# A fused vision tower on one core: order of the queues in the second attention layer

## The reference, cut to what matters

```python
qkv = x @ W_qkv + b_qkv
dots = jnp.einsum('bhid,bhjd->bhij', q, k) * dk ** (-0.5)
dots = dots * mask.astype(dots.dtype)
attn = jax.nn.softmax(dots, axis=-1)
out_attn = jnp.einsum('bhij,bhjd->bhid', attn, v)
out_attn = out_attn.transpose(0, 2, 1, 3).reshape(b, n, e) @ W_out + b_out
...
return w[0] * out_attn + w[1] * x_cema
```

## Time and profile before

| what | value |
|---|---|
| median of 3 runs | 828.24 us (827.29 to 828.71) |
| profiled execution, its own time | 827.36 us |
| its span in the trace | 825.6 us |
| busy: PE, DVE, ACT, POOL | 76%, 61%, 42%, 28% of the span |
| second attention in the trace | 589.5 to 749.9 us |

### The profile page before, as it was taken

One profiled execution on the slowest core, in us unless ns is written; L12 is line 12 of the kernel. 1 busy time (PEld: TensorE's weight loads), 2 busy tenths in 40 slices (PEclk: granted clock), 3 DMA queues, 4 the chain that ended last, 5 costly groups with the idle time before them and its releaser, 6 DMA issues. The chain is left out here.

```text
span 825.6 us, 21280 instructions
## 1 busy us (share of the span) xinstructions
PE 630.7 (76%) x8455; PEld 513.7 (62%) x8455; DVE 504.3 (61%) x904; ACT 348.7 (42%) x871; POOL 230.8 (28%) x254
## 2 busy tenths in 40 slices
PE   2999999999999996761399867858689999971002
PEld 1888888888888885541394546638567777761001
DVE  0376666666666666427222678759578888855862
ACT  0013444444444444422164333443167888865600
POOL 1263333333333333000000223330235555430001
PEclk9999999999999998665558997775579999995555
DMA  8443333333332300003980440000000000001300
GB/s 358 161 191 119 118 119 117 117 117 117 117 117 117 117 2 2 2 1 106 198 116 0 54 52 0 0 2 0 1 2 4 0 0 0 3 2 53 74 5 4
DMA packets 28659, 55.36 MB, mean 67 GB/s; under 512 B 12274, under 2 KB 25698, under 8 KB 26114
## 3 DMA queue, kind: packets, MB, share of 16 engines
q1 hardware_dynamic: 28515, 54.62, 22.1%
q0 software_dynamic: 96, 0.07, 0.0%
HBM read 48.14 MB, written 6.55 MB: 66 GB/s over the span
## 5 line engine op out<-in xcount | busy, mean ns | idle before, releaser
L375 PE MATMUL a_bank<-a_x,a_tok_w 128*128 128x256 f32 (+1 forms) x608 | 150.6, 390 | 15.7 <-DVE a_ht L555 15.7
L375 PEld LDWEIGHTS a_bank<-a_x,a_tok_w 128*128 128x128 f32 (+1 forms) x608 | 113.1, 192 | 37.3 <-DMA tables<-in_tables 15.7
L124 POOL TENSOR_TENSOR a_qt<-a_qp,data 128x512 f32<-128x512 f32 x64 | 71.8, 1153 | 2.1 <-POOL a_qp L617 1.6
L617 POOL TENSOR_TENSOR a_qp<-a_rope 128x260 f32<-128x260 f32 x16 | 11.7, 733 | 175.5 <-DVE a_rope L499 175.5
L282 ACT ACTIVATE a_at<-a_bank 65x256 f32<-65x256 f32 x128 | 38.9, 390 | 26.8 <-PE a_bank L259 26.8
L493 DVE SCALAR_TENSOR_TENSOR a_ht<-a_bank,data 128x256 f32<-128x256 f32 x16 | 7.7, 484 | 64.5 <-PE a_bank L375 64.5
L1449 POOL TENSOR_TENSOR b_e<-b_e,b_inv 128x585 f32<-128x585 f32 (+1 forms) x32 | 35.4, 1108 | 22.6 <-DVE b_inv L1299 22.6
L259 PE MATMUL a_bank<-a_mix,a_e 64*65 64x64 f32 x1024 | 41.5, 237 | 0.0
L259 PEld LDWEIGHTS a_bank<-a_mix,a_e 64*65 64x65 f32 x1024 | 36.9, 149 | 4.1 <-issue 3.4
L910 POOL COPY s_ycp<-yout 128x512 f32<-128x512 f32 (+1 forms) x16 | 11.5, 726 | 97.6 <-POOLq L829 93.5
L195 ACT ACTIVATE a_e<-a_e 128x390 f32<-128x390 f32 (+1 forms) x48 | 24.3, 510 | 33.2 <-DVE a_e L175 33.2
(11 more groups left out here) (251 smaller groups left out, 1520.2 us busy)
## 6 DMA issues: line engine op xcount, KB each, us to landing
a_x<-in_x SPq DMA_DIRECT2D x16, 2304.0 KB, 7.9
lag_rows<-r_kernel SPq DMA_DIRECT2D x1, 4192.5 KB, 38.8
lags<-lag_rows SPq DMA_DIRECT2D x1, 2112.5 KB
base<-places SPq DMA_DIRECT2D x1, 2080.0 KB
out<-e_plain SPq DMA_DIRECT2D x16, 130.0 KB
expert_weights<-in_w SPq DMA_DIRECT2D x2, 1024.0 KB, 5.9
a_tok_w<-in_tok_w SPq DMA_DIRECT2D x1, 1152.0 KB, 6.7
data<-in_data SPq DMA_DIRECT2D x1, 910.5 KB, 4.7
```

The source lines that it names most:

```text
L124: nc.gpsimd.tensor_tensor(qt[:, b * BLOCKS * P:(b + 1) * BLOCKS * P].rearrange("p (c h i) -> p c h i", i=qb, h=HEADS), wide(by_image[:, b, ...
L375: mm = nc.tensor.matmul(banks[0][:, 0:GP], w[0:rows, k * DIM:(k + 1) * DIM], x[p][0:rows, k * GP:(k + 1) * GP], start=(k == 0), stop=(k == ...
```

## The change

No instruction is added or removed and none changes its size. Three queues of `attend_causally` are reordered. On VectorE the row sums and reciprocals of the second half go ahead of the residual. On ScalarE the squares go ahead of the first exponential, that one ahead of the query tiles; the second query tile and the keys go behind the second exponential and the second `save_pair`; the attention output goes ahead of the mean. On GpSimd both `normalise` calls go ahead of `last_queries` and `centre`.

```diff
@@ VectorE
                     invert(g + 1, 0, e[1 - p])
+                    invert(g + 1, 1, e[1 - p])
                 if exists(g - 1):
                     residual(g - 1)
                     total_of_rows(g - 1)
-                if exists(g + 1):
-                    invert(g + 1, 1, e[1 - p])
@@ ScalarE
-            def queries_keys(g):
+            def queries(g, half):
                 act.wait_ge(S.q_done, g + 1)
                 wait_past(act, S.scores_done, g)
                 wait_past(act, S.last_ready, g)
-                for p in range(2):
-                    nc.scalar.activation(qm[:, p, :], ...)
+                nc.scalar.activation(qm[:, half, :], ...)
+
+            def keys(g):
                 act.wait_ge(S.k_done, g + 1)
                 nc.scalar.activation(kt[:, :], ...)
...
                 if exists(g - 2):
                     save_gates(g - 2)
-                if exists(g + 2):
-                    queries_keys(g + 2)
+                    squares(g - 2)
                 if exists(g + 1):
                     exponent(g + 1, 0, e[1 - p])
+                if exists(g + 2):
+                    queries(g + 2, 0)
+                if exists(g + 1):
+                    exponent(g + 1, 1, e[1 - p])
                 if exists(g):
                     save_pair(g, 1)
+                if exists(g + 2):
+                    queries(g + 2, 1)
+                    keys(g + 2)
                 if exists(g + 1):
-                    exponent(g + 1, 1, e[1 - p])
                     save_values(g + 1, 1 - p)
+                if exists(g):
+                    save_heads(nc, act, g, obank, ot, S)
                 if exists(g - 1):
                     average(g - 1)
-                if exists(g):
-                    save_heads(nc, act, g, obank, ot, S)
-                if exists(g - 2):
-                    squares(g - 2)
@@ GpSimd
             for g, i, p in pipeline(pool, 2, GROUPS + 1):
+                if exists(g + 1):
+                    normalise(g + 1, 0, e[1 - p])
+                    normalise(g + 1, 1, e[1 - p])
                 if exists(g + 2):
                     last_queries(g + 2)
-                if exists(g + 1):
-                    normalise(g + 1, 0, e[1 - p])
                 if exists(g - 1):
                     centre(g - 1)
-                if exists(g + 1):
-                    normalise(g + 1, 1, e[1 - p])
                 if exists(g + 2):
                     copy(g + 2, p)
```

More of the change, by code:

```diff
@@ L1350, in queries_keys @@
                 wait_past(act, S.last_ready, g)
-                for p in range(2):
-                    nc.scalar.activation(qm[:, p, :], sc[:, 0, 0:GT], ACT.Identity, bias=parity_bias[:, p:p + 1],
-                                         scale=T("parity")[:, p:p + 1]).then_inc(S.q_ready, 1)
+                nc.scalar.activation(qm[:, half, :], sc[:, 0, 0:GT], ACT.Identity, bias=parity_bias[:, half:half + 1],
+                                     scale=T("parity")[:, half:half + 1]).then_inc(S.q_ready, 1)
+            def keys(g):
                 act.wait_ge(S.k_done, g + 1)
```

## The result

The changed kernel takes 846.28 us (843.54 to 847.80, 4 runs) against 828.48 us for the kernel before (now 4 runs): a ratio of 1.0216, 95% interval 1.0198 to 1.0234. Slower, as forecast, but by 17.8 us and not 8.4, and above the top of the range, 844. The profiled execution took 846.50 us, its span is 844.7.

A forecast was written before the change was run, and what follows sets the result against it. In the second attention TensorE and VectorE were taken as nearly full at 8.48 us a step. The new ring's 9.3 gave 0.7 + 1.3 + 9.9 - 3.5 = +8.4 us: 836.6 against 828.24, range 832.5 to 844.

The forecast's parts named there:

- The ring: Second attention, mask to next mask through GpSimd's normalisations and last queries: 9.3 us a step instead of 8.48; chance 0.78.
- `last_queries` at 0.50, not 1.03: GpSimd's last queries in their new place: 0.50 us, since VectorE's new neighbours should not hold them up.
- The clock: TensorE's granted clock in the second attention: taken as full in every step, its fall left to a rival.
- the same ring, dearer: Rival: last queries stay at 1.03 or TensorE's clock drops, 0.5 us more a step, 843 to 844 us; chance 0.14.
- one of the prediction's own signs of being wrong: In the profile after: a granted clock under 1.00 between 620 and 730 us would show the forecast wrong.
- I charged 0.5 in every step: Price of a clock drop: scores about 0.5 us longer at half clock, over 14 steps 7 us.
- Values at 7.5, "with 0.6 to spare" at 8.1,: ScalarE saves values 7.5 us behind the mask; TensorE's scores start at 8.1 and find them ready.
- the fast rival: Rival: VectorE's stall is filled, GpSimd's queue doesn't decide, TensorE's 7.95 us bounds a step, 818 us; chance 0.05.
- "VectorE's mask waits for the scores 1.3 us": Expected sign in the profile after: VectorE's mask waits 1.3 us for TensorE's scores in every step.
- The ends: First and last steps of the second attention: +0.7 us at group 0, -3.5 after group 15's mask (bounds -2.3 and -4.5).
- The table load: ScalarE, group 0: the 1.28 us load before the first exponential should vanish behind waits; that step still +0.7.
- no change: Rival: the ring costs 0.3 us a step and the ends give it back, 828 us; chance 0.03.

The follow-up runs named there:

- e1: The changed kernel with GpSimd's order of before put back, VectorE's and ScalarE's new orders kept: 827.6 us, ratio to before 0.9996.
- e4: The changed kernel with last queries moved between the two normalisations on GpSimd: 826.25 us, ratio to before 0.9991.
- e8: The kernel before the change with VectorE's new order only: 850.80 us, ratio to before 1.0283.

## Why the prediction was right and where it failed

- **The ring was right.** Row sums, reciprocal, two normalisations in a row (2.18 for 2.17), last queries, scores: each link is there, the one from last queries to scores at 0.22 to 0.35 instead of 0.15. Steps at full clock are 9.25 to 9.54 where I wrote 9.3. With the clock held up by filling, the kernel takes 836.71 us, where the forecast was 836.6; that it agrees to a tenth is luck. The kernel before measured 827.50 us beside it, so the difference is 9.2 us and not 8.4.
- **`last_queries` at 0.50, not 1.03.** Right: 0.50 or 0.51 in all 16 groups. In the step shown it ran beside the row totals, in the next one beside the residual:

```profile
685.08 0.51 POOL L1444 TENSOR_TENSOR b_qlast<-b_qm,tables 128x128 f32<-128x128 f32 x1
...
685.18 0.75 DVE L1307 SCALAR_TENSOR_TENSOR b_z<-b_bank,blend,base 65x512 f32<-65x512 f32 x1 [1.53 <-PE b_bank L1189]
```

By the Trainium skill's rule on two SBUF inputs (GPSIMD Engine Reference, Key points) neither of these should hold it up (the residual reads one tile from PSUM and one from SBUF, the row totals read one), and the trace agrees with 0.50 and 0.51.
- **The clock is the step that failed.** The sum took full clock for every step and left its fall to a rival, "the same ring, dearer", with a chance of 14% that it shared with a slower `last_queries`. I compared a stretch with 1.97 us busy of 3.5, after which the clock fell, with 2.1 of 3.4 that I expected, and called mine "a bit better than that". That rested on TensorE standing still 1.3 us. In the step shown it stood 1.56, and 0.19 before attention times values, and was busy 1.65 of 3.40: less than in the stretch that I had compared it with, and the clock fell, to 0.86 on average from 620 to 730 us. This was one of the prediction's own signs of being wrong. The Trainium skill describes a loop whose waits bring the clock down in every pass (TensorE: Matmul & The Clock Gate, HAM oscillation). The trace agrees in part: four falls in twelve steps, each followed by a recovery, and not one in every pass.
- **And its price was too low.** I charged 0.5 in every step, for the scores alone. Against the 9.36 of the filled kernel, what came was 1.4 (once 2.7) in four steps of twelve, since in a cold step the whole path from the mask to the exponential is longer (10.75 instead of 9.36), and some 0.4 in the steps at whose end the clock fell. The mean is 10.06 less 9.36, 0.7 a step, 8.4 us over the twelve.
- **Values at 7.5, "with 0.6 to spare" at 8.1,** was right, and I didn't draw from it what it says: 9.3 less 0.6 is a second ring of 8.7, and e1 and e4 gave 8.70. So the fast rival's 7.95 a step was out of reach by the prediction's own figures, even with GpSimd out of the way.
- **"VectorE's mask waits for the scores 1.3 us"** was a slip: 1.3 was TensorE's idle time. VectorE has 7.3 us of work in 9.3, and where the clock stayed up its mask waited 1.90 (737.55, 746.80) and 2.07 (666.80).
- **The ends.** The table load ran at 595.42, 5 us ahead of its exponential, hidden as forecast (+0.7 for the step). The end of the stage gave 2.8 and not 3.5, inside its bounds.
- **The fast rival and no change** are out: from the mask of group 3 to that of group 15 no step of a kernel with GpSimd's new order was under 9.2, filled or not.

## What to carry to other kernels

Before moving an instruction behind others in an in-order queue, write down the ring that it belongs to (who waits for it, and what that work feeds one step later) and add it up; an engine that is idle half the time can still set the beat when its one urgent instruction stands behind two patient ones. A stall that such a ring puts on TensorE should be priced twice, once as time and once as a possible fall of its clock, and a trace whose steps all ran at full clock doesn't show the second. To part the two, fill the idle time with matmuls that nobody reads, sized by a duration from the trace.

## What the runs showed of the hardware

In the changed kernel TensorE stood still 1.52 to 1.61 us before seven of the scores between 624 and 716 us, each time at a granted clock of 1.00. Behind four of these waits the clock fell to about 0.5. Behind the three others (scores at 624.75, 656.03 and 665.48) it didn't, and waits of 0.7 to 0.9 us in steps of 8.7 (e1, e4) never brought it down between 620 and 730 us. So the length of the wait alone doesn't tell whether the clock falls; what else it takes, no run here shows. Two rows, the first without a fall behind it and the second with one:

```profile
665.48 0.91 PE L1166 MATMUL b_scores<-b_kt,b_qm 32*64 32x65 f32 x64 [1.52 <-POOL b_qlast L1444]
...
695.47 1.14 PE L1166 MATMUL b_scores<-b_kt,b_qm 32*64 32x65 f32 x64 [1.56 <-POOL b_qlast L1444]
```

In e8 GpSimd's plain copy took 0.87 us and VectorE's two-input subtraction 1.17 while they ran side by side, for 0.40 and 0.69 otherwise:

```profile
674.98 1.17 DVE L1283 TENSOR_TENSOR b_e<-b_e,b_mx 128x520 f32<-128x520 f32 x1
...
674.54 1.05 POOL L1448 TENSOR_TENSOR b_e<-b_e,b_inv 128x520 f32<-128x520 f32 x1
675.54 0.87 POOL L1433 COPY b_h<-h_feat 128x260 f32 x1
```

The subtraction began while GpSimd's normalisation still ran, which kept its usual 1.05, and the copy began while the subtraction ran. The rows fit an order in which each of the two stood behind the one before it: the subtraction ended 0.56 behind the normalisation, the copy 0.26 behind the subtraction. The durations repeat in the other steps of the loop (0.86 or 0.87, 1.14 to 1.17), but no run here tried this separately.
